# Taking the low parts of the output weights on GpSimd instead of VectorE, in a fused attention and feed-forward block

## The reference

```python
x = x + tanh(g_xattn) * (attention(layernorm(x), ctx) @ wo)   # 16 heads of 128, 4 key groups
x = x + tanh(g_ffn) * ffn(layernorm(x))                       # weights rounded to fp8 e4m3, 768 wide
```

## Time and profile before

| what | before |
|---|---|
| median of three runs | 336.58 us |
| the profiled execution | 338.61 us |
| its span, first to last instruction | 336.8 us |
| mean granted TensorE clock | 0.969 |
| TensorE busy | 295.1 us (88%) |
| VectorE busy | 234.7 us (70%) |
| ScalarE busy | 230.3 us (68%) |
| GpSimd busy | 180.7 us (54%) |

### The profile page before, as it was taken

The page is one execution under the profiler, slowest core; times in us unless marked ns, Lnnn a source line. Parts: engine busy times, 40 slices in busy tenths (PEclk is TensorE's granted clock), DMA queues, the critical chain, the costliest instruction groups (busy, mean ns, idle before and its releaser), DMA issues.

```text
span 336.8 us, 6878 instructions
## 1 busy us (share of the span) xinstructions
PE 295.1 (88%) x2288; PEld 243.5 (72%) x2288; DVE 234.7 (70%) x494; ACT 230.3 (68%) x890; POOL 180.7 (54%) x179
## 2 busy tenths in 40 slices
PE   3885994988399699999999899999999999998876
PEld 1334572877288588887888788878887888876764
DVE  1678599978997868755875587557766775566554
ACT  3377797464457577887788768877787768777622
POOL 1144475543486657744674568445854486456220
PEclk9997898799699999999999999999999999999999
DMA  6950514300000000000000000000000000000000
GB/s 195 370 179 23 230 62 140 95 16 1 2 1 3 6 12 16 2 2 2 18 16 0 16 0 16 0 0 0 16 2 0 1 18 3 0 3 17 2 0 33
DMA packets 6714, 12.76 MB, mean 38 GB/s; under 512 B 800, under 2 KB 4256, under 8 KB 6688
## 3 DMA queue, kind: packets, MB, share of 16 engines
q1 hardware_dynamic: 6688, 12.43, 10.7%
HBM read 11.38 MB, written 1.05 MB: 37 GB/s over the span
## 4 chain that ended last, share of the span: by engine, by line
PE 55%; DVE 18%; ACT 15%; issue 6%; POOL 2%; DMA 2%; SPq 1%; DVEq 0%; ACTq 0%; POOLq 0%
PE ps_kv L377 11%; PE ps_y L410 9%; PE ps_q L377 6%; PE ps_attn L617 6%; PE ps_scores L578 5%; PE ps_transposed L391 5%; PE ps_ff L440 4%; PE ps_probs L391 4%; ACT const L645 4%; PE ps_ff L460 3%; ACT probs L811 3%; DVE xt_lo L1054 2%; ACT values L672 2%; DMA const<-in_constants_dram 2%; DVE q_sin L929 2%
## 5 line engine op out<-in xcount | busy, mean ns | idle before, releaser
L811 ACT ACTIVATE probs<-ps_scores,exp_bias,q_scale 128x128 f32<-128x128 f32 x128 | 56.9, 456 | 32.0 <-DVE exp_bias L1072 31.9
L1192 POOL TENSOR_TENSOR q_rot<-q_rot,q_sin 128x512 f32<-128x512 f32 x32 | 41.3, 1290 | 25.6 <-DVE q_sin L929 25.5
L1149 POOL TENSOR_TENSOR q_scale<-ssq_eps,minus_half 128x4 f32<-128x4 f32 x32 | 37.5, 1173 | 18.8 <-DVE ssq_eps L1101 18.8
L1237 POOL TENSOR_TENSOR probs<-probs,row_inv 128x512 f32<-128x512 f32 x32 | 36.7, 1147 | 18.2 <-DVE row_inv L1133 18.0
L410 PE MATMUL ps_y<-w_o_hi,ot_hi 128*128 128x256 f32 x128 | 37.8, 296 | 7.9 <-DVE ot_lo L936 7.9
L1175 POOL TENSOR_TENSOR fuse_lo<-fuse,fuse_hi 128x256 fp32r<-128x256 f32 x21 | 15.3, 731 | 42.5 <-ACT fuse_hi L655 42.5
L645 ACT ACTIVATE const<-ps_q 128x128 bf16<-128x128 f32 x128 | 34.0, 292 | 6.0 <-PE ps_q L377 4.0
L410 PE MATMUL ps_y<-w_o_hi,ot_lo 128*128 128x256 f32 x128 | 36.4, 284 | 0.0
L410 PE MATMUL ps_y<-w_o_lo,ot_hi 128*128 128x256 f32 x128 | 36.4, 284 | 0.0
L578 PE MATMUL ps_scores<-kt,qt 128*64 128x128 f32 x512 | 34.2, 277 | 0.0
L617 PE MATMUL ps_attn<-pt,values 128*128 128x256 f32 x128 | 33.3, 383 | 0.0
(11 more groups left out here) (142 smaller groups left out, 885.1 us busy)
## 6 DMA issues: line engine op xcount, KB each, us to landing
stage<-in_wq_dram SPq DMA_DIRECT2D x4, 512.0 KB, 5.9
stage<-in_wo_dram SPq DMA_DIRECT2D x4, 512.0 KB, 4.7
ctx_t<-in_ctx_dram SPq DMA_DIRECT2D x8, 128.0 KB, 2.5
out_dram<-x SPq DMA_DIRECT2D x8, 128.0 KB, 1.7
x_sb<-in_x_dram SPq DMA_DIRECT2D x1, 768.0 KB, 6.7
stage<-in_gate_w_dram SPq DMA_DIRECT2D x2, 384.0 KB, 3.0
stage<-in_up_w_dram SPq DMA_DIRECT2D x2, 384.0 KB, 3.6
stage<-in_down_w_dram SPq DMA_DIRECT2D x2, 384.0 KB, 4.0
```

The lines of the kernel that those rows point to most:

```text
L811: last = nc.scalar.activation(probs[:, i, :], ps_s[:, i * P:(i + 1) * P], ACT.Exp, bias=exp_bias[:, i:i + 1], scale=q_scale[:, k % 2, i:i ...
L1149: return nc.gpsimd.tensor_tensor(dst, src, minus_half[:, 0:src.shape[1]], ALU.pow)
L1192: nc.gpsimd.tensor_tensor(q_rot[:, :, :], q_rot[:, :, :], q_sin[:, :, :], ALU.add)\
L1237: nc.gpsimd.tensor_tensor(probs[:, :, :], probs[:, :, :], row_inv[:, :].unsqueeze(2).broadcast_to([P, 4, P]), ALU.mult).then_inc(probs_rea ...
```

## The change

The low parts of the output weights are made on GpSimd. The new function stands at the end of GpSimd's step, right behind the product of the probabilities, and the order of the chunks stays that of `SPLIT_AT`; VectorE still makes the low parts of the other eight chunks. The semaphores are the same: GpSimd waits for `wo_hi_ready`, as VectorE did, and raises `wo_lo_ready`, for which TensorE and SP wait.

```diff
             def weight_lo(kind, i):
                 n = CHUNKS.index((kind, i))
-                if kind == "o":
-                    dve.wait_ge(wo_hi_ready, i + 1)
-                else:
-                    dve.wait_ge(w_hi_ready, SPLIT_ORDER.index((kind, i)) + 1)
-                hi, lo = {"kv": w_kv, "q": w_q, "o": w_o}[kind]
+                dve.wait_ge(w_hi_ready, SPLIT_ORDER.index((kind, i)) + 1)
+                hi, lo = {"kv": w_kv, "q": w_q}[kind]
                 nc.vector.tensor_tensor(lo[:, i].rearrange("p c n -> p (c n)"), staged(n, CHUNK_COLS),
                                         as_f32(hi[:, i].rearrange("p c n -> p (c n)")), ALU.subtract)\
-                    .then_inc(wo_lo_ready if kind == "o" else w_lo_ready, 1)
+                    .then_inc(w_lo_ready, 1)

             def split_weights(u, k):

                 for kind, i in SPLIT_AT.get(at_step(u, k), ()):
-                    weight_lo(kind, i)
+                    if kind != "o":
+                        weight_lo(kind, i)
...
+            def output_weight_lo(i):
+                n = CHUNKS.index(("o", i))
+                pool.wait_ge(wo_hi_ready, i + 1)
+                nc.gpsimd.tensor_tensor(w_o[1][:, i].rearrange("p c n -> p (c n)"), staged(n, CHUNK_COLS),
+                                        w_o[0][:, i].rearrange("p c n -> p (c n)").bitcast(f32), ALU.subtract)\
+                    .then_inc(wo_lo_ready, 1)
+
...
                     nc.gpsimd.tensor_tensor(probs[:, :, :], probs[:, :, :],
                                             row_inv[:, :].unsqueeze(2).broadcast_to([P, 4, P]), ALU.mult).then_inc(probs_ready, 1)
+
+                for kind, i in SPLIT_AT.get(at_step(u, k), ()):
+                    if kind == "o":
+                        output_weight_lo(i)
```

## The result

The changed kernel takes 342.47 us (median of four runs, 341.51 to 343.05), the kernel before 336.55 us on the same chip: ratio 1.0148 [1.0105, 1.0191]. It is slower, and above the range of 334.6 to 338.9 us. The profiled execution took 341.99 us, 3.4 more than that of before.

A forecast was written before the change was run, and what follows sets the result against it. VectorE was taken to decide in attention steps 1 to 3. Terms: 0 in step 1, -0.2 up to the projection, -0.3 taken in all, giving 338.3 us profiled and 336.3 us median; range 334.6 to 338.9 us.

The forecast's parts named there:

- the side that had 0.24: Whole kernel slower than can be told from no change, about 1.7 us; chance 0.24.
- its first rival: Step 2's moved subtraction starts before normalization xn; chain behind the projection 1.6 us later, 338.2 us; chance 0.31.
- The length of the pieces: Each moved 128x1024 subtraction takes 2.39 us on GpSimd.
- Step 1: Removed VectorE subtraction worth 0; moved one delays GpSimd's k_cos and q_rot, TensorE 1.2 us late but covered.
- Step 2: VectorE's saved 1.98 us is spent: 0.87 on a new ssq_eps wait, the rest waiting for k_sin.
- xn and piece 1: Step 3: xn meets step 2's moved subtraction within 0.01 us; xn first puts the projection at 59.05, -0.2 us.
- turn-taking: Between VectorE and GpSimd, the one that has waited goes next; held against the moved subtraction starting before xn.
- Step 3: Two moved subtractions fill GpSimd to 70.0 us; exp_bias of step 4 then comes between -0.5 and +0.3 us.
- the +0.3 case: End of step 3: q_rot goes before the second xt_lo, which ends at 71.7 us, +0.3 us.
- After step 7 nothing should differ: Sign to check: the changed kernel runs like the kernel before from there on.
- the clock case: TensorE's clock stays up behind the shortened pause before step 1's projection: -2.1 us, 334.5 us; chance 0.13.

The follow-up runs named there:

- the kernel with xn first: Changed kernel in which GpSimd also waits for VectorE's normalization xn of step 3 before starting step 2's moved subtraction: 337.29 us, ratio 1.0006.
- piece 1 alone: Changed kernel with only step 2's subtraction on GpSimd, the other three back on VectorE: 337.91 us, ratio 0.9983.
- Piece 0 alone: Changed kernel with only step 1's subtraction on GpSimd, the other three back on VectorE: 342.03 us, ratio 1.0111.
- pieces 0, 2 and 3: Changed kernel with step 2's subtraction back on VectorE, those of steps 1 and 3 on GpSimd: 341.68 us, ratio 1.0106.
- The delay put in step 7: Changed kernel with two extra VectorE reductions, some 1.1 us together, at the head of step 7: 342.55 us, ratio 1.0126.
- that in step 5: Kernel before with one extra VectorE reduction, some 0.56 us, at the head of step 5: 338.84 us, ratio 1.0044.
- the fill of step 3: Changed kernel with 20 unused transposes in TensorE's pause ahead of the output projection in step 3: 337.51 us, ratio 0.9997.
- that of step 8: Changed kernel with 24 unused transposes in TensorE's pause ahead of step 8's projection, TensorE's loop written out: 339.81 us, ratio 1.0056.
- Both fills: Unused transposes in TensorE's pauses of steps 3 and 8, loop written out: changed kernel 337.29 us, kernel before 335.94, step 3's two subtractions alone moved 335.63.
- In quarters: Changed kernel with each moved subtraction cut into four of 256 columns: 338.35 us, ratio 1.0031.

## Why the prediction was wrong

It gave 336.3 us and 0.61 for no change. The outcome lies on the side that had 0.24, and 4.3 us above the time that its first rival gave. Two terms failed: the wait of k_var behind piece 0, put at nothing, and the clock behind the pause of step 8, taken as given. Point by point:

**The length of the pieces: right.** Predicted 2.39 us, measured 2.34 and 2.37.

**Step 1: the failing step.** It said that piece 0 moves k_cos and q_rot, and that VectorE pays only in step 2, at exp_bias and ssq_eps. The first projection (0.35 us at 45.40, waiting for the piece) did come late and did cost nothing, as predicted: the kernel with xn first has it too and takes the time of the kernel before. But k_var was left out. It is four columns wide like exp_bias, which the text itself had priced as held. Before, it ran in the gap between GpSimd's instructions; now k_cos follows the piece with no gap and starts 0.01 us before it. It takes 1.31 us instead of 0.19, so it waits 1.1 us.

**Step 2: right in sum, wrong in part.** The new wait of 0.87 us at ssq_eps didn't come (0.17 us); k_var had taken its place. The wait of quant_m for k_sin came (1.40 us, 0.55 undisturbed). The sum of the quantization starts 10.03 us behind the reciprocal of step 1; predicted was "where it was", 10.04. The probabilities end at 12.87 by that clock, predicted 12.85.

**xn and piece 1: the rival came.** The text put xn at 12.86 us behind the reciprocal (12.88 measured) and the piece within 0.01 us of it. The piece went first by 0.04, xn took 2.45 us. The rival named this, its place and its length, and put the projection 17.5 us behind the reciprocal; it came at 17.18. The forecast had leant on turn-taking, but there was none to take: xn was not yet waiting when the probabilities ended, so that the piece simply started first. The Trainium skill ("SBUF — State Buffer", section "Who interferes with whom") lets the order of issue decide, and the trace agrees: 54.47 against 54.51. Piece 1 first was therefore worth more than the 0.31 it had.

**But that wait does not cost by itself.** The experiments show what neither case said. By the rival xn's wait costs 1.6 us; piece 1 alone has that wait and costs nothing, as it only replaces the subtraction. Piece 0 alone has no such wait and costs 1.0111. In the sum of the forecast the term for step 1 is the one that was mis-sized: 0, where the runs show 1.1 us of reach and about 0.9 to 1.35 us of time, before the clock.

**Step 3: the pieces longer, the gain not seen.** The two together took 5.41 us, where 4.8 was predicted, and ended 27.15 us behind the reciprocal of step 1 (predicted 26.6). The second xt_lo waited for q_rot, 1.38 us, the +0.3 case of the prediction.

**The clock: the largest miss.** The text treated the clock behind the pause as given, and had a rival only for its staying up. "After step 7 nothing should differ" is refuted: 2.7 us were lost there, with the same pause ahead. Its range added 0.7 us to the rival for longer pieces and nothing for the clock, though the profiled execution stood 2.0 us above the median with nothing edited. That gap was a sign that the time of this kernel varies with the low stretches of an execution: the 20 runs above 340 us all have a mean clock of 0.965, the fastest 0.984. The Trainium skill ("TensorE: Matmul & The Clock Gate", section "What's actually happening") calls the number of slow matmuls at the start of one kernel "run-variable". No run here counts those; the runs of before show the like for stretches in the middle of a kernel, over 5 us. What the other runs add is that a small delay can move nearly all runs to the bad end.

A slip beside these: the clock case is worked out as 334.5 us and enters the range as 334.6. Nothing hangs on it.

**Open.** Why the reach decides isn't settled. Of 28 runs of the three unfilled kernels with piece 0 and a reach of 17.0 us or more (the changed kernel, pieces 0, 2 and 3, and piece 0 alone), 27 were above 341 us; of 122 of the kernel before, none was above 341.2, and 20 were above 340. The pause of step 8 is as long in both. The delay put in step 7 cost nothing that can be measured and that in step 5 between 0.3 and 2.7 us, so a delay doesn't cost 4 to 5 us wherever it stands. That a pause filled in step 3 also left the clock up in step 8 in one profile, and that the fill of step 3 wins back all and that of step 8 half, may mean that what the clock did before matters; no run here varied that by itself. Nor does a run free k_var alone and leave the pieces where they are: that its wait is piece 0's price is read from the profiles.

## What to carry to other kernels

When work moves to the other engine of a pair that locks out, list every instruction of the first engine that may now meet it, the four-column ones too, and ask where the instruction taken away had stood: ahead of a wait it was free, and the moved copy can only cost. Where two starts come within a tenth of a microsecond, price both orders. Where the times of one kernel spread with the granted clock, put the price of one more low stretch (2.9 us here) into the range of any edit that moves TensorE's pauses, and try filling the pauses.

## What of the hardware was unexpected

- An instruction that waits can pay for nearly the whole of the other engine's, however small it is: k_var, four columns wide, took 1.31 us against 0.19; xn took 2.45 against 0.40. In quarters the same piece cost xn 0.83 and took 2.83 us instead of 2.34.
- GpSimd's small inverse roots hardly disturb VectorE: ssq_eps took 0.17 us at 48.14, and w_q_lo its undisturbed 1.22 from 48.50, while k_inv and then k_sin ran or waited.
- 20 unused transposes, 2.35 us of TensorE's idle time, made the changed kernel 5.2 us quicker. Both fills, with TensorE's loop written out, brought the kernel before to 0.9954 [0.9921, 0.9987] of its time.
- The same 20 transposes came too late in one execution: the clock had fallen as they began (0.57 over 56 to 60 us), and they took 3.75 us.
- The clock in the pause of step 8 was 1.00 in one profile of the kernel before and fell in the other, behind pauses of 3.09 us in both.
